# Scanning in half blocks of 64 channels with sums in two column halves, a residual added on TensorE, and a new slot table

## What is computed

```python
x = layernorm(h)                                   # 205 x 1024
xp = x @ x_proj_w.T                                # 32 + 16 (B) + 16 (C) columns
dt = softplus(xp[:, :32] @ dt_proj_w.T + dt_proj_b)
h_t = exp(dt_t * A) * h_(t-1) + dt_t * B_t * x_t   # scan over 205 positions, 1024 channels x 16 states
y_t = sum_n h_t[n] * C_t[n] + D * x_t
h = h + y                                          # first residual
z = layernorm(h)
h = h + (z @ w.T + bias)                           # w from 4 bit codes, or 8 bit codes where |z| > 64
```

## Time and profile before

| | us |
|---|---|
| median of three runs | 6210.84 |
| profiled execution | 6212.96 |
| its span | 6211.1 |
| mean granted TensorE clock | 0.978 of full |
| PE, DVE, ACT, POOL busy | 5793.1, 5698.9, 5123.3, 5709.9 |

### The profile page before, as it was taken

The page is one execution under the profiler, slowest core; times in us unless marked ns, Lnnn a source line. Parts: engine busy times, 40 slices in busy tenths (PEclk is TensorE's granted clock), DMA queues, the critical chain, the costliest instruction groups (busy, mean ns, idle before and its releaser), DMA issues. The chain is left out here.

```text
span 6211.1 us, 111922 instructions
## 1 busy us (share of the span) xinstructions
PE 5793.1 (93%) x35091; PEld 5384.9 (87%) x35091; DVE 5698.9 (92%) x4564; ACT 5123.3 (82%) x12831; POOL 5709.9 (92%) x3484
## 2 busy tenths in 40 slices
PE   4676999999999999999999999999999999999998
PEld 3545899999999999999999999999999999999997
DVE  8776999999999999999999999999999999999996
ACT  5716888888888888888888888888888888888884
POOL 4526999999999999999999999999999999999995
PEclk9887999999999999999999999999999999999999
DMA  4701221222122211222122212221222112221220
GB/s 94 160 2 66 83 82 61 77 88 87 60 77 86 88 71 68 83 88 77 61 83 88 82 62 77 88 83 61 77 88 88 68 71 83 88 77 61 83 82 34
DMA packets 115881, 478.49 MB, mean 77 GB/s; under 512 B 17441, under 2 KB 52401, under 8 KB 107122
## 3 DMA queue, kind: packets, MB, share of 16 engines
q1 hardware_dynamic: 115314, 471.10, 22.0%
HBM read 327.82 MB, written 143.24 MB: 76 GB/s over the span
## 5 line engine op out<-in xcount | busy, mean ns | idle before, releaser
L1103 POOL TENSOR_TENSOR s_ring<-s_bc,s_u_t 128x820 f32<-128x820 f32 x2048 | 3618.3, 1788 | 4.4 <-DMA s_bc<-rows_bc 4.4
L999 ACT ACTIVATE s_decay<-s_dt_t,a_neg 128x205 f32<-128x205 f32 x8192 | 3047.3, 420 | 418.4 <-DVE s_ring L1164 346.7
L895 PE MATMUL s_y_ps<-s_ring,ident 128*128 128x205 f32 x16384 | 3140.5, 341 | 115.3 <-issue 61.6
L895 PEld LDWEIGHTS s_y_ps<-s_ring,ident 128*128 128x128 f32 x16384 | 2863.3, 191 | 207.4 <-POOL s_ring L1109 115.4
L1158 DVE TENSOR_TENSOR_SCAN s_decay<-s_decay,s_ring 128x820 f32<-128x820 f32 x1216 | 2265.0, 1863 | 192.9 <-ACT s_decay L999 178.9
L1109 POOL TENSOR_TENSOR s_ring<-s_ring,s_bc 128x820 f32<-128x820 f32 x832 | 1605.3, 1929 | 78.3 <-DVE s_ring L1158 78.2
L1158 DVE TENSOR_TENSOR_SCAN s_ring<-s_decay,s_ring 128x820 f32<-128x820 f32 x832 | 1542.8, 1854 | 41.9 <-ACT s_decay L999 41.1
L928 PE MATMUL s_xch<-s_x_t,w_low 128*128 128x205 f32 x8192 | 1524.3, 338 | 0.5 <-ACT s_x_t L1042 0.2
L928 PEld LDWEIGHTS s_xch<-s_x_t,w_low 128*128 128x128 f32 x8192 | 1422.6, 190 | 35.3 <-issue 30.5
L1164 DVE TENSOR_TENSOR s_ring<-s_decay,s_bc 128x820 f32<-128x820 f32 x1216 | 1229.5, 1011 | 41.8
L889 PE MATMUL s_y_ps<-s_x_t,s_d_diag 128*128 128x205 f32 x1024 | 279.1, 354 | 35.2 <-ACT s_x_t L1037 35.2
(11 more groups left out here) (165 smaller groups left out, 4223.5 us busy)
## 6 DMA issues: line engine op xcount, KB each, us to landing
s_bc<-rows_bc SPq DMA_DIRECT2D x64, 3280.0 KB, 11.0
mixed<-t_res SPq DMA_DIRECT2D x32, 1024.0 KB, 9.6
s_x_in<-mixed SPq DMA_DIRECT2D x64, 512.0 KB
s_h<-mixed SPq DMA_DIRECT2D x64, 512.0 KB
before<-s_h SPq DMA_DIRECT2D x64, 512.0 KB
out<-s_h SPq DMA_DIRECT2D x64, 512.0 KB
s_x_in<-in_txt SPq DMA_DIRECT2D x64, 308.0 KB
s_h<-in_txt SPq DMA_DIRECT2D x64, 308.0 KB
```

Of the source, the lines that this page charges most:

```text
L895: last = nc.tensor.matmul(y_ps, ident[:, :], ring[:, c % RING, n * LEN:(n + 1) * LEN], start=False, stop=(c % 4 == 3 and n == CN - 1))
L999: last = A.activation(decay[s % 2][:, n * LEN:(n + 1) * LEN], dt_t[:, par, j, :], ACT.Exp, scale=t["a_neg"][:, j, n0 + n:n0 + n + 1])
L1103: nc.gpsimd.tensor_tensor(ring[:, s % RING, :].rearrange("p (n l) -> p n l", n=CN), bc[:, par, n0:n0 + CN, :], u_t[:, j, :].unsqueeze(1).b ...
```

## The change

Line numbers of functions shift; the parts are these.

- **Half blocks.** A chunk is now 64 channels and eight states: partitions 0 to 63 hold the even states, 64 to 127 the odd ones, four of each along the free axis. There are still 32 chunks of 820 columns. B and C are laid out the same way, so `bc` is half as wide and comes in two DMAs.
- **Sums.** PE sums chunks in pairs, every other slot, four chunks behind (`SUM_LAG`). The stationary matrix is `stack` (128 x 64, two identities on top of each other); chunk c goes to PSUM partitions 0 to 63 and chunk c+1 to 64 to 127. The D product is cut in two in the same way.
- **dt and dt*x.** They are made in full blocks as before, in `dt_n` and `u_n`, and SP copies them into the half-block buffers `dt_t` and `u_t`: four DMAs for each of four pairs of blocks, for both, 32 an item. The first column of `dt_t` is set once at the start, and the `reset` stages go.
- **First residual.** PE adds h1 in PSUM with an identity product of 512 columns and the four transposed blocks behind it; ACT copies the result to h1 and takes the row sums along. DVE's `add` goes, and so does ACT's pass over h1 for the mean of layer norm 2.
- **Tables.** `ON_DVE` has 20 chunks instead of 19; the slots of all four engines are new, and SP's order is now a table, `SP_ORDER`.

```diff
-ON_DVE = (1, 3, 4, 5, 7, 9, 11, 13, 14, 15, 17, 19, 21, 23, 24, 25, 27, 29, 31)
+ON_DVE = (1, 2, 3, 4, 5, 7, 8, 10, 11, 13, 15, 16, 17, 19, 21, 23, 25, 26, 29, 31)
+SP_ORDER = [("u_hi", 2), ("u_hi", 3), ("spread", 0), ("steps", 0), ("steps", 1), ("write", 0), ("steps", 2), ("u_lo", 0),
+            ("load_rows", 0), ("u_lo", 1), ("keep", 0), ("steps", 3), ("load", 0)]
...
+            def halves(target, place, source, r, first, signal):
+
+                for i in range(2):
+                    for h in range(2):
+                        sp.dma_start(target[64 * i:64 * i + 64, place + h:place + 4:2, first:],
+                                     source[64 * h:64 * h + 64, 2 * r:2 * r + 2, first:]).then_inc(signal, 16)
+
+            def steps(v, par, r):
+
+
+                wait(sp, p_empty, v * P_USES + r + 2)
+                halves(dt_t, dt_place(par, 4 * r), dt_n, r, 1, dt_in[r])
...
-                if "turn1" in groups and ahead:
-                    load(u + 2, x)
...
+                for name, arg in SP_ORDER:
...
+                    if name == "load" and "turn1" in groups and ahead:
+                        load(u + 2, x)
...
+                    if name == "steps" and "turn1" in groups:
+                        steps(u + 1, 1 - par, arg)
...
                 for n in range(CN):
-                    last = nc.tensor.matmul(y_ps, ident[:, :], ring[:, c % RING, n * LEN:(n + 1) * LEN],
-                                            start=False, stop=(c % 4 == 3 and n == CN - 1))
-                last.then_inc(sum_done, 1)
+                    for h in range(2):
+                        last = nc.tensor.matmul(y_ps[sides[h], :], t["stack"][:, :], ring[:, (c + h) % RING, n * LEN:(n + 1) * LEN],
+                                                start=False, stop=(c % 4 == 2 and n == CN - 1))
...
+                nc.tensor.matmul(bank[0:rows(k), :], ident[0:rows(k), 0:rows(k)], h1[0:rows(k), par, k, 512 * side:512 * side + 512],
+                                 start=True, stop=False)
                 for j in range(4):
-                    last = nc.tensor.transpose(bank[0:rows(k), P * j:P * j + P], x_t[:, par, 4 * side + j, cols(k)], ident[:, :])
+                    last = nc.tensor.matmul(bank[0:rows(k), P * j:P * j + P], x_t[:, par, 4 * side + j, cols(k)], ident[:, :], start=False, stop=(j == 3))
...
+                A.activation(h1[0:rows(k), par, k, 512 * side:512 * side + 512], bank[0:rows(k), :], ACT.Copy,
+                             accum_out=half_sum[0:rows(k), k, side:side + 1]).then_inc(empty, 1)
```

More of the change, by code:

```diff
@@ L837, in spread @@
                 wait(sp, spread_out, v * 16 + 16)
-                sp.dma_start(bc[:, par, :, :], rows_bc[par:par + 1, :, :].broadcast_to([P, 2 * NS, LEN])).then_inc(bc_in[par], 16)
-            def entry(u, par, x, groups, ahead=True):
-                if "add" in groups:
-                    keep(u - 1, 1 - par, x)
-                if "turn1" in groups and ahead:
-                    load(u + 2, x)
[L845 to L850, removed]
+                for i in range(2):
+                    sp.dma_start(bc[64 * i:64 * i + 64, par, :, :],
+                                 rows_bc[par:par + 1, i::2, :].broadcast_to([64, 2 * NK, LEN])).then_inc(bc_in[par], 16)
@@ new lines, in inputs @@
+            def inputs(v, r):
+                wait(sp, u_done, v * 4 + r + 1)
+                halves(u_t, 4 * r, u_n, r, 0, u_in[r])
+            def entry(u, par, x, groups, ahead=True):
+                for name, arg in SP_ORDER:
+                    if name == "keep" and "add" in groups:
+                        keep(u - 1, 1 - par, x)
+                    if name == "load" and "turn1" in groups and ahead:
+                        load(u + 2, x)
+                    if name == "spread" and "turn1" in groups:
+                        spread(u + 1, 1 - par)
+                    if name == "write" and "out_low" in groups:
+                        write(u - 2, par, x)
+                    if name == "load_rows" and (not isinstance(u, int) or 0 <= u < BATCH):
+                        load_rows(u, par)
+                    if name == "steps" and "turn1" in groups:
+                        steps(u + 1, 1 - par, arg)
+                    if name == "u_lo" and "turn1" in groups:
+                        inputs(u + 1, arg)
+                    if name == "u_hi" and (not isinstance(u, int) or 0 <= u < BATCH):
+                        inputs(u, arg)
@@ L884, in sums @@
                 j = c // 4
+                sides = [slice(64 * h, 64 * h + 64) for h in range(2)]
                 if c % 4 == 0:
@@ L1008, in mean @@
                 n = rows(k)
+                minus_mean = t["ln_in"][0:n, which - 1, 0, k:k + 1]
                 if which == 1:
                     wait(act, loaded, v * 32 + 32)
+                    A.activation(xn[0:n, k, :], x_in[0:n, k, :], ACT.Copy, accum_out=ln_sum[0:n, k:k + 1]).then_inc(ln_piece[which], 1)
+                    wait(act, ln_piece[which], v * LN_DONE + PIECE[which]["mean", k, 0])
+                    A.activation(minus_mean, ln_sum[0:n, k:k + 1], ACT.Copy, scale=-1.0 / DIM).then_inc(ln_piece[which], 1)
                 else:
@@ L1032, in var, with add @@
                 A.activation(ve, total, ACT.Identity, scale=1.0 / DIM, bias=t["eps_ln"][0:n, :]).then_inc(ln_piece[which], 1)
+            def add(v, par, r, x):
+                k, side = r // 2, r % 2
+                bank, empty = take(x, "add", r)
+                A.activation(h1[0:rows(k), par, k, 512 * side:512 * side + 512], bank[0:rows(k), :], ACT.Copy,
+                             accum_out=half_sum[0:rows(k), k, side:side + 1]).then_inc(empty, 1)
             def block_output(u, par, j, x):
@@ L1194, in finish @@
                                 h1[0:rows(k), par, k, 512 * side:512 * side + 512], ALU.add).then_inc(empty, 1)
[L1196 removed]
+            stages = {"dt": dt_total,
                       "out_low": lambda v, par, k, x: finish("out_low", v, par, k, x),
```

174 lines of the change are left out of this document (93 added, 81 removed), and 6 rows, old and new, of the table ACT_PLAN.

## The result

| | before | after |
|---|---|---|
| median, us | 6210.76 (6207.64 to 6211.06, 4 runs) | 6759.22 (6754.8 to 6764.27, 4 runs) |
| ratio, 95% interval | | 1.0883 (1.087 to 1.0896) |
| profiled span, us | 6211.1 | 6758.0 |
| one item, us | 87.97 | 96.67 |

The change costs 548 us, 8.8%. I had forecast +225. The direction and the place were right, the size was not: 6759 lies above the range that ended at 6640.

What follows compares the result with a forecast made beforehand. PE, DVE and POOL were at their limit before; DVE would bound it after: 82.1 work + 7.1 stop + 2.4 idle = 91.6 against 87.97 us, +3.6 over 62 items, +225, 6436 us; 8-in-10 range 6290 to 6640.

Steps and rivals of the forecast that it cites:

- The engines' work: Work per item after the change: DVE 82.1, POOL 84.3, ACT 76.5 us; PE 69, or 72 with tile switches.
- the doubled D products: On PE: D products cut in two cost nothing if column halves run side by side, otherwise +2.8 us an item.
- tile switches: On PE: some 28 changes of tile shape an item, about 0.1 us each, together 3 us.
- The halves: In PE's sums: the two column halves run side by side, taking 22.3 us an item off 44.6.
- the halves in line: Rival: column halves don't run side by side on PE; PE 94 us, item +8.5, kernel 6740 us; chance 0.06.
- The rival of the weight loads: On PE: only 64-column weight loads stand in line; PE 88.3 us, item some +1, kernel 6500 us; chance 0.04.
- The wait that comes: At each item's end: ACT's `mean1` waits for the late x_in load; DVE stands still 7.1 us (5.3 to 10).
- D: End of DVE's `dt_total` in slot 31; the x_in load was forecast issued at D + 1.8, landing at D + 6.1.
- Bandwidth is not the question: On DMA: 32 new copies, 3.3 MB an item, judged no bandwidth problem at a DMA share of 0.22.
- Other idle time: DVE's idle time outside the item's end: 3.4 us an item before, forecast 2.4 (1.0 to 3.4).
- The clock: PE's granted clock might fall as PE pauses at each item's end; put into the upper range, not the sum.
- The faster rival: At the item's end: x_in lands within 2.5 us of D; item 86.6 us, kernel 6126 us; chance 0.10.

## Why the prediction was wrong in size

*The engines' work* was right: DVE, POOL and ACT within 0.3 us. PE was 77.0, not 72; with the load early it is 75.5, at 88% busy. I had put the doubled D products at nothing: they went from 4.3 to 5.2 us an item. My 3 us for tile switches stay open, as no run separates them.

*The halves* were right: the sums fell by 49.0 - 27.2 = 21.8 us of busy time, where I had forecast 22.3. (My 44.6 for the sums before was their number times the distance of two starts; their busy time was 49.0.) The rivals on them fall: PE would need 94 us an item with the halves in line and 88.3 with the weight loads in line, and it needs 75.5 with the load early. The rival of the weight loads put a pair of records at 0.171 + 0.137 = 0.31 us; pairs start every 0.174. With them falls, for these tiles, the reading of the Trainium skill (TensorE: Matmul & The Clock Gate, Part 3) that a weight load overlaps products in flight only when the row group differs: both halves lie on the same 128 rows.

*The wait that comes* is the step that failed, in its size. As forecast, all of ACT's decays stand behind `mean1`, and DVE stops right behind chunk 0. I gave the stop 7.1 us; it was 11.8 on average (11.64 behind chunk 0 in the item shown), above my upper bound of 10, and the item missed by 96.7 - 91.6 = 5.1. Its terms, from D, in the item shown:
- SP would be free at D. It was busy until D + 1.6, with kept rows behind four copies of u. The order of SP shown with the change has these copies there; I had not counted them.
- Four dt copies at 0.41, the price of a plain load in straight code. They took 3.39 / 4 = 0.85; the copies of u 2.56 / 4 = 0.64. The load was issued at D + 5.2 (mean 5.5), not D + 1.8.
- 4.2 us of transfer, measured where the load had the engines to itself. It was 5.4 after its issue behind copies (mean 5.3), of which much is the longer issue of the load itself, 1.22 us instead of 0.35; 9.0 on average when the copies were issued behind it; 4.7 where there were none.

`mean1` thus began at D + 10.6, not D + 6.1. These 4.5 us (4.7 in the means) are also what the stop is too long by, and more than the 3 us that I had allowed at most for slow copies and kept rows. I had read the order of SP's instructions, but only as a chain of issues. "Bandwidth is not the question" was said of the mean share, 0.22; at the place that mattered 2.5 MB stood in a row, and the share was 0.53 to 0.91 for 10 us. At 245 GB/s, 2.5 MB are 10.2 us.

*Other idle time* was 96.7 - 81.9 - 11.8 = 3.0 against 2.4: near. *The clock* fell to half after the stops, as I had feared for PE, and at other pauses of PE too. What it cost isn't separated here; PE's work is 1.5 us an item more with the stops than without, and DVE's other idle time 0.6 more than forecast.

*The faster rival* needed the load to land by 2.5 us after D, and in the kernel after it did not. Its time is what the kernel takes once its load stands where nothing waits: 86.2 an item against its 86.6.

## What to carry over

When a table moves a transfer behind an instruction that comes late, price it by everything that the same queue issues there, bytes and all, and not by the transfer's own time measured elsewhere. A DMA share averaged over a loop says nothing about the 10 us at its end. One item's end is a sample: in the one shown with the load ahead of dt the issue came 1.3 us after D, and the mean was 2.1. And before a large change is called good or bad, move its latest load to the front: here one entry in a list was 653 us, and hid a gain of 102.

## What the runs showed of the chip

- A copy from one SBUF buffer to another of 64 x 2 x 204 floats (about 104 KB, rows of 816 bytes) holds SP for 0.61 us (median), four in a row for 2.4; at the item's end of the kernel after four of dt take 3.4 on average, 4.6 at worst. A load of 128 rows of 4 KB holds it for 0.33 to 0.38 when free; behind such copies it was 0.38 in some items and up to 1.60 in others.
- A load of 0.84 MB reached its reader 4.7 us after its issue with nothing else in flight, 5.3 behind four copies, and 9.0 with kept rows ahead of it and four copies behind it (means of 47 or 48).
- Two fp32 products of 128 rows and 64 columns go side by side on the same rows: in alternation a pair of records starts every 0.174 us, its two 3 to 14 ns from each other; eight records in a row to one half start 0.174 apart, until the other half's turn comes and its first four run beside the last four. Busy time a record of 205 columns is 0.107 us in alternation, 0.144 with four in a row, 0.191 for full width before.
